# A side network's ten weighted sums begun by ScalarE, and its items in another spacing

## What is computed

```python
# layer 0, four times:
p = leaky_relu(points, 0.01)
points = (w_center @ p + sum over 8 neighbours of w_neighbor @ p) / 9 + points
# layer 1, for every point and each of its 30 neighbours:
sph = [rho, theta, phi]                        # sqrt, arctan2, arctan2
feat = concatenate([sph, sph - mean(sph)])     # 6 features
h = lrelu(bn(feat @ W1.T))                     # 6 channels
h = lrelu(bn(h @ W2.T))                        # 3 channels
h = lrelu(bn(h @ W3.T))                        # 1 channel
att = softmax(h over the 30 neighbours)
out = x + sum over neighbours of att * x[neighbour]
```

## Time and profile before

| | us |
|---|---|
| median of 3 runs | 791.47 (790.16 to 792.34) |
| the profiled execution | 791.82 |
| its span in the trace | 789.9 |
| TensorE matmul busy | 742.2 (94%) |
| VectorE busy | 631.9 (80%) |
| ScalarE busy | 254.7 (32%) |
| GpSimd busy | 204.0 (26%) |

### The profile page before, as it was taken

The page is one execution under the profiler, slowest core; times in us unless marked ns, Lnnn a source line. Parts: engine busy times, 40 slices in busy tenths (PEclk is TensorE's granted clock), DMA queues, the critical chain, the costliest instruction groups (busy, mean ns, idle before and its releaser), DMA issues.

```text
span 789.9 us, 13131 instructions
## 1 busy us (share of the span) xinstructions
PE 742.2 (94%) x5530; PEld 604.1 (76%) x5530; DVE 631.9 (80%) x943; ACT 254.7 (32%) x415; POOL 204.0 (26%) x158
## 2 busy tenths in 40 slices
PE   5879899798999999999999999898899898999998
PEld 4668788776778887888878888686687787777776
DVE  4777999949999999999998789867754877778741
ACT  7325553521363121210010344433444233333220
POOL 3112867780321301301220161450262000000000
PEclk9989999989999999999999999999999999999999
DMA  9620003001002000255442000000000000010101
GB/s 356 180 106 2 1 1 107 1 28 80 1 0 101 8 2 2 78 175 178 152 152 77 1 1 0 1 0 1 0 1 1 1 1 2 28 41 29 41 27 54
DMA packets 21179, 39.87 MB, mean 50 GB/s; under 512 B 10112, under 2 KB 10112, under 8 KB 20864
## 3 DMA queue, kind: packets, MB, share of 16 engines
q1 hardware_dynamic: 20976, 36.93, 13.4%
q10 hardware_dynamic: 144, 2.10, 0.7%
HBM read 32.59 MB, written 6.42 MB: 49 GB/s over the span
## 4 chain that ended last, share of the span: by engine, by line
PE 71%; DVE 17%; ACT 4%; issue 3%; POOL 3%; DMA 1%; SPq 0%; POOLq 0%; DVEq 0%; ACTq 0%
PE bank L1425 26%; PE bank L1449 5%; PE bank L1560 4%; PE bank L1404 4%; PE bank L1405 4%; PE bank L1406 4%; PE bank L1510 4%; PE bank L1561 4%; PE bank L1562 4%; PE bank L1323 3%; PE bank L1324 3%; PE bank L1325 3%; DVE pts_l L920 2%; DVE idx L848 2%; DVE vals L846 2%
## 5 line engine op out<-in xcount | busy, mean ns | idle before, releaser
L1425 PE MATMUL bank<-nbr,pts_l 128*128 128x512 f32 x1024 | 246.8, 400 | 7.5 <-DVE pts_l L920 7.3
L1425 PEld LDWEIGHTS bank<-nbr,pts_l 128*128 128x128 f32 x1024 | 194.6, 192 | 51.1 <-DVE pts_l L920 10.4
L462 POOL TENSOR_TENSOR pts_h<-scratch,pts_h 128x512 fp32r<-128x512 f32 x58 | 78.8, 1364 | 166.3 <-ACT pts_h L657 166.3
L1404 PE MATMUL bank<-wT,pts_h 128*128 128x512 f32 x256 | 105.4, 412 | 8.9 <-DVE pts_l L920 4.8
L1405 PE MATMUL bank<-wT,pts_h 128*128 128x512 f32 x256 | 102.8, 402 | 0.0
L1406 PE MATMUL bank<-wT,pts_h 128*128 128x512 f32 x256 | 102.4, 400 | 0.0
L1323 PE MATMUL bank<-pts_h 128*128 128x512 f32 (+2 forms) x192 | 72.8, 379 | 14.2 <-DVE pts_l L819 10.5
L664 ACT CAST pts_l<-bank 128x512 fp32r<-128x512 f32 x64 | 37.5, 588 | 138.6 <-PE bank L1406 138.5
L657 ACT CAST pts_h<-scratch 128x512 fp32r<-128x512 f32 x58 | 35.6, 616 | 131.2 <-DVE scratch L915 127.4
L1324 PE MATMUL bank<-pts_l,pts_h 128*128 128x512 f32 (+2 forms) x192 | 69.3, 361 | 0.0
L1325 PE MATMUL bank<-pts_h,pts_l 128*128 128x512 f32 (+2 forms) x192 | 69.2, 360 | 0.0
(11 more groups left out here) (205 smaller groups left out, 1249.9 us busy)
## 6 DMA issues: line engine op xcount, KB each, us to landing
more<-a_rows SPq DMA_DIRECT2D x17, 480.0 KB, 4.4
scratch<-a_rows SPq DMA_DIRECT2D x15, 480.0 KB, 4.2
X<-in_ctx SPq DMA_DIRECT2D x12, 512.0 KB, 6.5
out_dram<-X SPq DMA_DIRECT2D x16, 256.0 KB, 2.0
more<-in_ctx SPq DMA_DIRECT2D x4, 512.0 KB, 7.0
scratch<-in_fside_BxSxS SPq DMA_DIRECT2D x2, 1024.0 KB, 12.4
w_keep<-wT SPq DMA_DIRECT2D x1, 2048.0 KB, 6.3
X<-in_x SPq DMA_DIRECT2D x2, 1024.0 KB, 6.7
```

The costliest lines, as they stand in the source:

```text
L462: pool.tensor_tensor(p_l[:, t, hf * HALF:(hf + 1) * HALF], p32(n), p_h[:, t, hf * HALF:(hf + 1) * HALF].bitcast(F32), ALU.subtract).then_i ...
L1404: pe.matmul(bank[g % 3][:], p_h[:, t, cols], wT[:, 0, t, :], start=(t == 0), stop=False)
L1425: mm = pe.matmul(bank[3 + g % 3][:], y[:, m, t * P:(t + 1) * P], nbr[b][:, m, hf * HALF:(hf + 1) * HALF], start=(m == 0 and part_ == 0), s ...
```

## The change

Three things change; what is computed stays the same.

1. The first term of each of the ten weighted sums is made by ScalarE (`first_term`, an activation that copies with a scale) into the same half of `tmp`. VectorE's `mix` begins with its second term and waits for `first_term_ready`. A new semaphore, `weighted_sum_step`, tells ScalarE when the map that it reads is final and the half of `tmp` that it writes is free.
2. The items are spaced anew. Steps 82 to 95 now hold (9,2), 10, 11, 12, 13, 14, (15,16), (21,0), (17,18), (21,1), (19,20), 22, 24, 25, and steps 96 to 113 hold 26, 27, 28, (29,31), 30, 32, (33,34), 35, 37, 38, 39, 40, (41,42), 44, 45, 46, 47, 48. Steps 70 to 81 are as before. The table is one entry longer and `T0` is counted with one less, so it stays 114. The statistics of the six maps are taken in three parts of two instead of two parts of three.
3. VectorE's first `leaky` waits for three of the six maps of `bn_apply` instead of all six.

```diff
         NET = [(0,), (1,), (2,), (3, 4), ((5, 0),), ((5, 1),), ((5, 2),), (6,), (7,), (8,), ((9, 0),), ((9, 1),),
-               ((9, 2), 10), (11,), (12, 13), (14,), (15,), (16,), (17,), (18,), (19,), (20,), (21,), (22,), (),
-               (24, 25), (26,), (27, 28), (29, 30), (31,), (32, 33), (34,), (35,), (), (37, 38), (39,), (40,), (41, 42),
-               (), (44, 45), (46,), (47,), (48,)]
+               ((9, 2),), (10,), (11,), (12,), (13,), (14,), (15, 16), ((21, 0),), (17, 18), ((21, 1),), (19, 20), (22,),
+               (24,), (25,), (26,), (27,), (28,), (29, 31), (30,), (32,), (33, 34), (35,), (37,), (38,), (39,), (40,),
+               (41, 42), (44,), (45,), (46,), (47,), (48,)]
+
+        MIXED = (2, 3, 4, 5, 6, 7, 9, 10, 11, 13)
+        FIRST_NEEDS = (1, 1, 2, 3, 4, 5, 8, 8, 9, 12)
...
-        T0 = M0 + len(NET) + 1
+        T0 = M0 + len(NET)
...
+            def first_term(n):
+
+                act.wait_ge(s_mix, FIRST_NEEDS[n])
+                if n < 6:
+                    c, src, w = n, 10, w_eff[:, n, 0:1]
+                elif n < 9:
+                    c, src, w = n - 6, 0, prm[:, 48 + 6 * (n - 6):49 + 6 * (n - 6)]
+                else:
+                    c, src, w = 0, 6, prm[:, 72:73]
+                act.activation(tmp[:, c % 2], slots(src), ACT.Copy, scale=w).then_inc(s_first, 1)
...
+                    if m == 14:
+                        first_term(0)
+                        first_term(1)
+                    if m in ((21, 0), (21, 1)):
+                        first_term(2 * m[1] + 2)
+                        first_term(2 * m[1] + 3)
+                    if m == 28:
+                        first_term(6)
+                        first_term(7)
+                    if m == 32:
+                        first_term(8)
+                    if m == 40:
+                        first_term(9)
...
                     if j == 0 and first:
-                        ts(acc, slots(a), w(j), ALU.mult)
+                        dve.wait_ge(s_first, n + 1)
+                    elif j < len(src) - 1:
+                        stt(acc, slots(a), w(j), acc, ALU.mult, ALU.add)
+                    elif last:
+                        dve.scalar_tensor_tensor(slots(dst), slots(a), w(j), acc, ALU.mult,
+                                                 ALU.add).then_inc(s_mix, 1)
+                        dve.wait_ge(s_mix, MIXED[n])
                     else:
-                        stt(slots(dst) if last and j == len(src) - 1 else acc, slots(a), w(j), acc, ALU.mult, ALU.add)
+                        stt(acc, slots(a), w(j), acc, ALU.mult, ALU.add)
...
-            def leaky(first, n, ev):
-                dve.wait_ge(s_act, DONE[ev])
+            def leaky(first, n, ev, left=0, step=0):
+
+                dve.wait_ge(s_act, DONE[ev] - left)
                 h = slots(first, n)
-                stt(h, h, SLOPE1, h, ALU.mult, ALU.max)
+                if not step:
+                    stt(h, h, SLOPE1, h, ALU.mult, ALU.max)
+                    return
+                dve.scalar_tensor_tensor(h, h, SLOPE1, h, ALU.mult, ALU.max).then_inc(s_mix, 1)
+                dve.wait_ge(s_mix, step)
...
                 if n == 27:
-                    leaky(0, 3, "bn1a")
+                    leaky(0, 3, "bn1a", 3, 8)
```

More of the change, by code:

```diff
@@ L236, in build @@
         s_tab = sem("table_ready")
+        s_first = sem("first_term_ready")
+        s_mix = sem("weighted_sum_step")
         s_mlp = sem("mlp_to_act")
@@ L972, in stt, with mix @@
                 link(dve.scalar_tensor_tensor(o, a, s_, b_, op0, op1))
-            def mix(c, dst, src, w, first=True, last=True):
+            def mix(n, c, dst, src, w, first=True, last=True):
                 acc = tmp[:, c % 2]
@@ L1090, in network @@
                     ts(tmp, Y, 0.0, ALU.is_ge, 2.0, ALU.mult)
-                    stt(A, tmp, -1.0, A, ALU.add, ALU.mult)
+                    dve.scalar_tensor_tensor(A, tmp, -1.0, A, ALU.add, ALU.mult).then_inc(s_mix, 1)
+                    dve.wait_ge(s_mix, 1)
                 if n in range(15, 21):
                     c = n - 15
-                    mix(c, c, (10, 6, 7), lambda j: w_eff[:, c, j:j + 1])
-                if n == 21:
-                    bn_partial(0, 6, range(3), False)
+                    mix(c, c, c, (10, 6, 7), lambda j: w_eff[:, c, j:j + 1])
+                if n in ((21, 0), (21, 1)):
+                    bn_partial(0, 6, range(2 * n[1], 2 * n[1] + 2), False)
                 if n == 22:
-                    bn_partial(0, 6, range(3, 6), True)
+                    bn_partial(0, 6, range(4, 6), True)
                 if n == 25:
@@ L1108, in network @@
                     c, hf = (n - 29) // 2, (n - 29) % 2
-                    mix(c, 6 + c, range(3 * hf, 3 * hf + 3),
+                    mix(6 + c, c, 6 + c, range(3 * hf, 3 * hf + 3),
                         lambda j: prm[:, 48 + 6 * c + 3 * hf + j:49 + 6 * c + 3 * hf + j], hf == 0, hf == 1)
@@ L1117, in network @@
                 if n == 40:
-                    leaky(6, 3, "bn2a")
+                    leaky(6, 3, "bn2a", 0, 12)
                 if n == 41:
-                    mix(0, 0, (6, 7, 8), lambda j: prm[:, 72 + j:73 + j])
+                    mix(9, 0, 0, (6, 7, 8), lambda j: prm[:, 72 + j:73 + j])
                 if n == 42:
```

## The result

| | before | after |
|---|---|---|
| median, first series | 791.29 us (4 runs, 790.16 to 792.34) | 782.57 us (4 runs, 780.24 to 785.04) |
| the profiled execution | 791.82 | 784.69 |
| span | 789.9 | 782.6 |
| mean granted clock of it | 0.972 | 0.976 |

The ratio is 0.989, interval 0.9848 to 0.9933. The four times of the changed kernel are 784.69, 780.45, 785.04 and 780.24: two levels. Each run lists its mean granted clock: 0.976 and 0.974 for the upper two, 0.982 for both lower ones. The program is the same and the times go with the clock, so a part of the result belongs to the clock and not to the change. The median, 782.57, lies between the two levels, where no run is.

A forecast was written before the change was run, and what follows sets the result against it. TensorE bounds the kernel, so only VectorE or ScalarE work it waits for counts. 6.2 us gained by iteration 6's last pair, less 0.6 for half clock, gives 5.6: 786.0 us forecast, range 783.5 to 789.1.

The forecast's parts named there:

- the two places: Iterations 5 and 6, where the first aggregation step's last matmul pair waits for the eighth `y_low`; last pair of 6: 6.2 earlier.
- the better case: Rival: no long half clock in iteration 6, or first terms wait less; 784.0 to 785, without any drop 783.6; chance 0.12.
- clock, table and spacing cases: Rivals: half clock stays in iteration 5 (787.7, 0.10), table loads cost more (788.6, 0.06), VectorE not relieved (788.2, 0.05).
- Place one: Iteration 5, first aggregation step's last matmul pair: TensorE waits about 1.0 instead of 4.1 us, gain 3.2, full clock after.
- Pair to pair: From the last matmul pair of iteration 5's first aggregation step to iteration 6's: 6.2 gained there, including 3.2 from iteration 5.
- The start of the rectifier: Iteration 6: the first rectifier, waiting for three maps instead of six, starts at 534.2 against 539.23 before.
- the 1.0 behind the second `y_high`: Iteration 6: the second rectifier stands behind a `y_low` whose `y_high` waits for all six applications, adding 1.0 us.
- Half clock behind place two: Iteration 6, after gaps of about 2 and 4 us: half clock costs 2.3 instead of 1.7, giving back 0.6.
- The table load costs its row: Against the rival that arctangent and square root loads each hold ScalarE another 1.28 us: 788.6, chance 0.06.
- Half clock did not stay in place one: Against the rival that iteration 5's gap of 1.0 still brings half clock: 787.7 at full price, chance 0.10.
- ScalarE's queue did not slip: Against the rival that late sums make ScalarE hold back pieces in iteration 6, 3.65 each time: 793.3, chance 0.04.
- The change does not relieve VectorE: Rival: VectorE waits for each first term as long as computing it; 2.2 come back in iteration 6: 788.2, chance 0.05.

The follow-up runs named there:

- spacing_only: Changed kernel with all ten first terms back on VectorE, keeping the new spacing and shorter rectifier wait: 785.16 us, against 790.88 for the kernel before.
- stats_late: Changed kernel with the second layer's statistics one step later, behind iteration 6's eighth low half: 778.80 us, ratio to before 0.9869.
- pieces_first: Changed kernel with ScalarE's first two pairs of first terms behind the first pieces, not ahead of them: 785.86 us, against 789.79 for the kernel before.

## Why the prediction was right or wrong

**Wrong: the number.** Forecast 786.0 with a range from 783.5; measured 782.57. The direction and the mechanism in the two places were right. The step that failed is the lower end of the range: "without any drop there ... 783.6", and a range that takes in "the better case and most of the clock, table and spacing cases". All of them priced the half clock only where the change works; what it does in the rest of the span stood in the sum at nothing, and no reason was given. The trace before loses 22 us in all (its mean clock of 0.972 over 789.9 us), some 5 of them in the three stretches of the two places, and I took the other 17 as a constant. The runs show that it isn't one. The mean clock of the changed kernel went from 0.972 to 0.982 and its times from 787.80 to 780.24; the kernel before had 0.970 to 0.987 and 793.93 to 783.82. That is 7.6 and 10.1 us for unchanged programs. Two of the first four runs had 0.982, near 780.3, and these put the median outside. In the later series, of 5 and 12 runs, the medians 784.59 and 784.88 lie in the range, 1.4 and 1.1 below the forecast. So that the first median missed the range was bad luck in part; that the range had no room for it was not.

**The sum, against the profiled execution.** Forecast 5.6, so 786.2 for it, measured 7.13 and 784.69, by the ledger above:
- Place one: forecast 3.2, measured 3.08. A gap of 1.0 was forecast and is 0.98; the arctangent's wait of 1.3 is 1.33; the clock was to stay full and did. Iteration 6 began 4.6 us earlier than before, with the 0.89 put back (525.99 + 0.89 against 531.47), where I had 4.8.
- Pair to pair: 6.2 - 3.2 = 3.0 forecast, 3.81 measured. The start of the rectifier was right (534.2 less the 0.89 that all lies earlier is 533.3; it is 533.27). So was the 1.0 behind the second `y_high` (0.92). The pieces began 2.5 later than before, with the 0.89 put back (500.18 + 0.89 - 498.54), where I had 2.8; a first term costs 0.62, where I had taken 0.70 with 0.6 as the lower bound. The 0.7 that is left is behind the rectifier: 23.3 us to the eighth low half, where I had 24.0. Of it 0.5 is one tiny instruction of the kernel before that took 0.66 us in the 25.2 from which I started; the changed kernel's took 0.17. The row of before, then the row of after:

```profile
561.94 0.66 DVE L967 TENSOR_SCALAR stat<-small 128x3 f32<-128x3 f32 x1
```

```profile
555.20 0.17 DVE L996 TENSOR_SCALAR stat<-small 128x3 f32<-128x3 f32 x1
```

- Half clock behind place two: 2.3 forecast, 2.3 measured, against 1.7 before. The gaps ahead of it were 1.51 and 3.27, not 2 and 4. (In the row of before that I read, the 1.59 us stand ahead of the last pair but one, at 563.86; the last pair follows at 564.40 without a gap of its own.)
- Upstream: nothing forecast, 0.89 measured, in unchanged code: the clock again, one stretch of half clock.

**The rivals.** The table load costs its row: the square root began 529.13 - 527.84 = 1.29 after its load, with nothing in between. The Trainium skill's 1.38 us of drain ("ScalarE: Activation LUTs", "What ACT_TABLE_LOAD costs") does not show here either, though the load now stood on the path. Half clock did not stay in place one. ScalarE's queue did not slip: the second pair of first terms waited for no sum. "The change does not relieve VectorE" was wrong as a mechanism, since each product was there in time; but its lesson holds, for `spacing_only` shows that the spacing, with the shorter wait, brings nearly everything: 5.7 of 6.3 us by the medians. The better case, 0.12, was the nearest to what was measured, and for another reason than it gave: the half clock in place two was just what the forecast had.

**The page on the clock.** By the Trainium skill, "TensorE: Matmul & The Clock Gate", section "Why this matters for your kernels", only idle gaps over about 3 us are to be avoided. The traces disagree, as the prediction had it: behind gaps of 1.59, 2.07 and 2.13 us in the trace before the clock is halved. And one of 2.2 us near 190 us is followed by half clock in the changed kernel's trace and not in that of `stats_late`. So my own rule, that 1.3 is safe and 1.6 isn't, was too sharp as well: the size of a gap alone does not decide.

## What to carry to other kernels

Where a side computation runs in slots beside a main line, look for the one point where the slack of the buffers ends, and move work from before it to after it; here 3.4 us of statistics moved by one step brought 3.5 us in the place (and 6.1 by the medians, with a better clock), while ten instructions handed to an idle engine brought about 1. Before a few tenths of a per cent are believed, compare the mean clock of the runs beside the times, and measure the place itself between two events of the trace. A range for such a kernel must hold the clock's spread over the whole span, not only at the gaps that the change touches.

## What the runs showed of the hardware

Runs of one unchanged program differ by over 5 us, and their times follow the mean granted clock: 783.82 at 0.987 against 789.3 at 0.976 and 792.1 at 0.972 for the kernel before, in one series. Two gaps of TensorE, 2.05 us ahead of the first one-hot product and 2.2 us near 190 us, were each followed by a stretch at 1.2 GHz in some traces and by none in others, at the same instruction and the same length. So removing a gap gives back its length in the place, and the 1.7 us of a stretch behind it only often; `pieces_first` took 1.7 us out of the place and its runs still became longer.

A tiny VectorE instruction can take several times as long as its neighbours, and which one it is was the same in every trace of a program. The first 128x3 one behind the second layer's statistics (L996) took 0.17 us in all five traces of the changed kernel and 0.75 in that of `stats_late`, which only moves it to another step. A 128x6 one (L1038) took 1.08 to 1.11 in those five and 0.17 in the trace of `pieces_first`. Nothing here shows why.
